# A vision block with a mixture of experts: shared network's first products from two fp32r parts, gates and state in place, three weights parted early

## What is computed

```python
h = attention(x)                        # 16 heads, softmax, output projection
h = concatenate([cls_tok, h])           # one class row in front of each sequence
h = h + state_space(layernorm(h))       # a linear recurrence over the rows, then C and D
u2 = layernorm(h)
shared = (silu(u2 @ Wg_s.T) * (u2 @ Wu_s.T)) @ Wd_s.T      # 256 -> 512 -> 256
p = sigmoid(u2 @ Wr.T + rb); two best of 8 experts
out = h + shared + sum(p_e * expert_e(u2))                 # experts of the same form as shared
```

## Time and profile before

| | |
|---|---|
| median of 3 runs | 1178.23 us (1177.75 to 1178.30) |
| the profiled execution | 1178.34 us, its span 1176.7 us |
| PE busy | 1131.6 us, 96% of the span |
| DVE busy | 908.8 us, 77% |
| ACT busy | 580.9 us, 49% |
| POOL busy | 400.1 us, 34% |
| mixing, from `make_y(1)` to `make_y(7)` | 543.49 to 761.68 us, six steps |

### The profile page before, as it was taken

The page is one execution under the profiler, slowest core; times in us unless marked ns, Lnnn a source line. Parts: engine busy times, 40 slices in busy tenths (PEclk is TensorE's granted clock), DMA queues, the critical chain, the costliest instruction groups (busy, mean ns, idle before and its releaser), DMA issues.

```text
span 1176.7 us, 21838 instructions
## 1 busy us (share of the span) xinstructions
PE 1131.6 (96%) x5894; PEld 685.5 (58%) x5895; DVE 908.8 (77%) x1557; ACT 580.9 (49%) x963; POOL 400.1 (34%) x516
## 2 busy tenths in 40 slices
PE   6998999999999999999999999987999999999996
PEld 3654333333333333466566766556888888888885
DVE  3788888888888888588877877777777777777775
ACT  3444777777777777632232221423444444444442
POOL 3011630101111010204345333464555555555553
PEclk9998999999999999999999999998999999999998
DMA  8886232323323232041244422411333333333332
GB/s 280 280 254 209 72 103 70 105 73 95 100 70 103 71 99 82 19 148 53 70 108 108 90 59 68 90 37 41 55 54 54 54 54 54 54 54 54 54 54 32
DMA packets 108690, 105.36 MB, mean 90 GB/s; under 512 B 42464, under 2 KB 97904, under 8 KB 108624
## 3 DMA queue, kind: packets, MB, share of 16 engines
q1 hardware_dynamic: 90528, 81.18, 24.2%
q0 software_dynamic: 18112, 23.57, 11.4%
HBM read 64.88 MB, written 39.68 MB: 89 GB/s over the span
## 4 chain that ended last, share of the span: by engine, by line
PE 79%; DVE 8%; issue 1%; ACT 1%; DMA 0%; POOL 0%; POOLq 0%; DVEq 0%
PE mix_pairs L73 17%; PE by_key L662 11%; PE pv L673 11%; PE by_query L653 9%; PE mix_made L1781 8%; PE mix_pairs L1251 5%; PE mix_pairs L1260 4%; PE mix_turn L1768 3%; PE mix_made L1236 2%; PE mix_made L1207 2%; PE mix_turn L1748 1%; PE mix_turn L1191 1%; PE by_query L694 1%; PE mix_made L1224 1%; DVE wu_rest L899 1%
## 5 line engine op out<-in xcount | busy, mean ns | idle before, releaser
L746 DVE TENSOR_REDUCE k_neg_max<-by_query 128x2 f32<-128x1024 f32 x240 | 282.9, 1220 | 54.7 <-PE by_query L653 54.0
L806 ACT ACTIVATE k_wu_e<-by_key 128x512 f32<-128x512 f32 x512 | 278.5, 601 | 84.0 <-PE by_key L662 80.5
L662 PE MATMUL by_key<-k_wg_e 99*128 99x512 bf16 x512 | 180.5, 386 | 3.1 <-DVE pv L782 3.0
L1724 POOL DMA_INDIRECT out_rows<-x_y,k_slot x72 | 113.9, 1582 | 157.7 <-PE mix_turn L1748 92.5
L653 PE MATMUL by_query<-k_wg_e 96*128 96x512 bf16 x480 | 145.0, 383 | 0.2
L1823 ACT ACTIVATE x_gate<-mix_pairs 128x512 f32<-128x512 f32 x72 | 43.0, 597 | 200.3 <-PE mix_pairs L73 200.3
L673 PE MATMUL pv<-k_wu_e,k_wd_e 128*17 128x512 f32 x1024 | 134.5, 598 | 0.3 <-ACT k_wu_e L806 0.3
L662 PEld LDWEIGHTS by_key<-k_wg_e 99*128 99x128 bf16 x512 | 42.4, 97 | 144.3 <-ACT k_wu_e L806 81.0
L73 PE MATMUL mix_pairs<-w_short,x_T 128*128 x288 | 121.8, 423 | 2.1 <-issue 2.1
L1781 PEld LDWEIGHTS mix_made<-x_wd,x_acts_T 128*128 128x128 f32 x864 | 111.2, 188 | 7.3 <-ACT x_acts_T L1845 0.9
L73 PE MATMUL mix_pairs<-w_short,x_rest 128*128 x288 | 114.8, 399 | 0.0
(11 more groups left out here) (234 smaller groups left out, 1851.9 us busy)
## 6 DMA issues: line engine op xcount, KB each, us to landing
k_wg_e<-kept_qk SPq DMA_DIRECT2D x384, 64.0 KB, 2.1
kept_qk<-k_qk_parts SPq DMA_DIRECT2D x32, 384.0 KB, 3.5
kept_v<-k_v_ones SPq DMA_DIRECT2D x8, 544.0 KB, 5.5
k_wd_e<-kept_v SPq DMA_DIRECT2D x32, 136.0 KB, 2.6
k_wu_e<-in_xT POOLq DMA_DIRECT2D x8, 512.0 KB, 6.2
kept_heads<-k_wd_e SPq DMA_DIRECT2D x8, 512.0 KB, 2.9
k_heads_in<-kept_heads SPq DMA_DIRECT2D x8, 512.0 KB
k_wg_e<-in_wg_e SPq DMA_DIRECT2D x8, 512.0 KB, 4.6
```

The source lines that it names most:

```text
L662: pe.matmul(by_key[:, key_bank(job), :], k_rows[0:SROWS, g, h, kt * P:(kt + 1) * P], q_rows[0:SROWS, g, h, :], start=True, stop=True).then ...
L746: dve.tensor_reduce(neg_max[:, g % 2, 2 * n:2 * n + 2], by_query[:, bank:bank + 2, :], AX.X, ALU.max, negate=True).then_inc(query_read, 1)
L806: act.activation(probs[:, key_tile(j) // 2 * G + j // 2 % G, j % 2, :], by_key[:, key_bank(job), :], ACT.Exp, scale=float(HD) ** -0.5).the ...
L1724: pool.indirect_dma_start(out=dram["out"], in_=y[:, r % 2, :], in_offset=None, compute_op=ALU.add, out_offset=bass.IndirectOffsetOnAxis(ap ...
```

## The change

- `shared_up` takes `u2` and the shared weights in two fp32r parts: 12 records per chunk in place of 8. It gets two waits (`w_s_cut`, `u2_cut`).
- ACT makes `u2_short` straight from PSUM (`copy_turned`), DVE makes `u2_rest` by `cut_second`, also from PSUM, and only then ACT makes the fp32 `u2_T`, which the router still needs; the logits wait for both, since they are written where the transposed u2 lay.
- Once, in step 0: ACT shortens the two shared weights (2 x [128, 2, 512]), DVE cuts them, behind `first_sum(1)` and ahead of `class_add`.
- `act_T` is gone: `shared_act` writes over `gate`, and silu now waits for `down_made` of the batch before. `state` is gone: the scans write over `back`, and `make_hidden` has its products in another order; their number is the same.
- `EARLY` is 3: pieces 0 to 2 in steps 1 to 3. In step 7 ACT shortens 3 to 10 and DVE cuts 3 and 4; in step 8 DVE cuts 5 to 15, eleven pieces; ACT shortens 11 between silu 1 and silu 2 and 12 to 15 behind silu 3.
- Some semaphores are joined (`choice_steps`, `dma_begun`); buffers lie elsewhere.

```diff
-EARLY = 4
+EARLY = 3
@@ stage_mix
-        act_T = sb("mix_act_T", [P, FC, S], FP32)
+        w_s_short = sb("w_s_short", [P, 2, DC, F], FP32)
+        w_s_rest, w_s = mem["w_s_rest"], (mem["wg_s"], mem["wu_s"])
@@ scalar
             def silu(j, m):
                 act.wait_ge(ev["gate_made"], FC * j + m + 1)
-                act.wait_ge(ev["act_done"], FC * j)
+                act.wait_ge(ev["down_made"], 2 * j)
...
                 if last:
                     act.wait_ge(mem["experts_in"], 16 * 3 * (E - 2))
+                    shorten_weights(act, mem, 3)
+                    act.wait_ge(ev["out_made"], 2 * B)
                     shorten_weights(act, mem, 4)
-                    act.wait_ge(ev["out_made"], 2 * B)
-                    shorten_weights(act, mem, 5)
+                if not this:
+                    act.wait_ge(ev["u2_stored"], 16 * B)
+                    shorten_weights(act, mem, 11)
...
-                    for n in (6, 7, 8):
+                    for n in (5, 6, 7):
...
-                    act.wait_ge(ev["state_done"], 2 * B)
-                    shorten_weights(act, mem, 9)
                     act.wait_ge(ev["y_made"], 2 * B)
-                    for n in (10, 11, 12):
+                    for n in (8, 9, 10):
...
                 if this:
+                    copy_turned(short(u2_short), b, "u2_turned", "shared_shortened")
+                    act.wait_ge(ev["u2_cut"], b + 1)
                     copy_turned(u2_T, b, "u2_turned", "u2T_copied")
...
                 if not this:
-                    act.wait_ge(ev["u2_stored"], 16 * B)
                     act.wait_ge(ev["logits_made"], B)
-                    for n in (13, 14, 15):
+                    for n in (12, 13, 14, 15):
...
+            for n in range(2):
+                act.activation(short(w_s_short[:, n, :, :]), w_s[n][:, :, :], ACT.Copy).then_inc(ev["shared_shortened"], 1)
             batches(act, step)
@@ tensor, shared_up
                 if m == 0:
                     pe.wait_ge(ev["acc_done"], 2 * j)
+                    pe.wait_ge(ev["w_s_cut"], 2)
+                    pe.wait_ge(ev["u2_cut"], j + 1)
...
-                        mm = pe.matmul(pairs[:, m % 2, n, :], w[:, c, m * P:(m + 1) * P], u2_T[:, c, :],
-                                       start=(c == 0), stop=(c == DC - 1))
+                        mm = split_products(pe, pairs[:, m % 2, n, :],
+                                            (w_s_short[:, n, c, m * P:(m + 1) * P], w_s_rest[:, n, c, m * P:(m + 1) * P]),
+                                            (u2_short[:, c, :], u2_rest[:, c, :]), start=(c == 0), stop=(c == DC - 1))
@@ tensor, step
                     pe.wait_ge(ev["u2T_copied"], b + 1)
+                    pe.wait_ge(ev["u2_cut"], b + 1)
@@ vector
-                dve.tensor_tensor(act_T[:, m, :], gate[:, m, :], pairs[:, m % 2, 1, :], ALU.mult).then_inc(ev["act_done"], 1)
+                dve.tensor_tensor(gate[:, m, :], gate[:, m, :], pairs[:, m % 2, 1, :], ALU.mult).then_inc(ev["act_done"], 1)
...
+            def cut_second(b):
+                dve.wait_ge(ev["shared_shortened"], 2 + b + 1)
+                dve.tensor_tensor(short(u2_rest[:, :, :]), turn[:, :, :], u2_short[:, :, :],
+                                  ALU.subtract).then_inc(ev["u2_cut"], 1)
...
-                scan(dve.tensor_tensor_scan(state[:, 0, :], back[0], back[1], mem["state0"][:, 0:1],
+                scan(dve.tensor_tensor_scan(back[0], back[0], back[1], mem["state0"][:, 0:1],
                                             ALU.add, ALU.add), wait=False)
...
-                dve.tensor_tensor(back[0], state[:, 0, :], cos, ALU.mult)
-                scan(dve.tensor_tensor(back[1], state[:, 1, :], sin, ALU.mult))
                 dve.wait_ge(ev["y_made"], 2 * b)
-                dve.tensor_tensor(hidden[:, 0, :], back[0], back[1], ALU.subtract).then_inc(ev["state_done"], 1)
...
+                dve.tensor_tensor(back[1], back[2], sin, ALU.mult)
+                scan(dve.tensor_tensor(hidden[:, 0, :], back[0], cos, ALU.mult))
+                dve.tensor_tensor(hidden[:, 0, :], hidden[:, 0, :], back[1], ALU.subtract).then_inc(ev["state_done"], 1)
...
                     if not this:
-                        for n in (6, 7, 8, 9):
+                        for n in (5, 6, 7, 8):
                             cut_weights(dve, mem, n)
...
                     shared_add(b - 1, 1 - par, 1)
                     if not this:
-                        for n in range(13, 2 * E):
+                        for n in range(12, 2 * E):
                             cut_weights(dve, mem, n)
+                if this:
+                    cut_second(b)
                 if nxt:
                     first_sum(b + 1)
                 if not prev:
+                    dve.wait_ge(ev["cls_up"], 1)
+                    for n in range(2):
+                        dve.wait_ge(ev["shared_shortened"], n + 1)
+                        dve.tensor_tensor(short(w_s_rest[:, n, :, :]), w_s[n][:, :, :], w_s_short[:, n, :, :],
+                                          ALU.subtract).then_inc(ev["w_s_cut"], 1)
+                if not prev:
                     class_add()
                 if this and not nxt:
-                    for n in (4, 5):
+                    for n in (3, 4):
                         cut_weights(dve, mem, n)
```

More of the change, by code:

```diff
@@ L928, in stage_mix @@
         by_feature = "p (c t) n -> p c (t n)"
-        heads_T, u_T, state, hidden, u2_T = (mem["mix_" + n][:, :, :].rearrange(by_feature, c=DC)
-                                             for n in ("heads_T", "u_T", "state", "hidden", "u2_T"))
+        heads_T, u_T, hidden, u2_T, u2_short, u2_rest = (
+            mem[n][:, :, :].rearrange(by_feature, c=DC)
+            for n in ("mix_heads_T", "mix_u_T", "mix_hidden", "mix_u2_T", "u2_short", "u2_rest"))
         h2 = sb("mix_h2", [P, 2, TT, D], FP32)
@@ L1467, in step @@
                     dve.wait_ge(ev["sigmoid"], b)
-                    top_two(dve, chain(dve, ev["top_steps"], TOP_STEPS * (b - 1)), mem, probs[:, :, :], TT)
+                    top_two(dve, chain(dve, ev["choice_steps"], (TOP_STEPS + SLOT_STEPS + 2) * (b - 1)), mem, probs[:, :, :], TT)
                     dve.tensor_tensor(chosen[:, 0:TT, :], mem["hot"][:, :, 0, :], mem["hot"][:, :, 1, :],
@@ L1506, in step @@
                     if not this:
-                        for n in (10, 11, 12):
+                        for n in (9, 10, 11):
                             cut_weights(dve, mem, n)
@@ L1709, in gather @@
                 pool.wait_ge(ev["x_turned"], R * i + r - X + 1)
[L1710 removed]
+            pool.sem_inc(mem["dma_begun"])
             gather_x(pool, mem, dram, r)
@@ L1983, in program @@
                "ev_cut": {n: sem("weights_" + n) for n in ("shortened", "rest_made")},
-               "tiles_listed": sem("tiles_listed"), "adds_listed": sem("adds_listed"), "slot_in": [sem(f"slot_in{r}") for r in range(RING)],
+               "tiles_listed": sem("tiles_listed"), "dma_begun": sem("dma_begun"), "adds_listed": sem("adds_listed"), "slot_in": [sem(f"slot_in{r}") for r in range(RING)],
                "x_gathered": [sem(f"x_gathered{r}") for r in range(FIRST_X)]}
```

44 lines of the change are left out of this document (22 added, 22 removed).

## The result

Changed kernel: 1179.9 us, the median of 20 runs (1178.43 to 1182.62). Kernel before, on the same chip: 1178.38 us, the median of 20 runs (1175.98 to 1179.83). The ratio is 1.0015, with a 95% interval of 1.0008 to 1.0022. So it is slower by 1.5 us, inside the 0.2% that was counted as no change. The profiled execution took 1180.8 us, 0.9 above the median; its span is 1179.1.

A forecast was written before the change was run, and what follows sets the result against it. Each mixing step's cycle was taken to run through both PE and DVE, with only chunk 1 on it. Sum: 1178.34 + 5.7 + 2.0 - 8.1 + 3.3 = 1181.2 us; forecast's own range 1179.0 to 1183.5, overall 1174.8 to 1186.0.

The forecast's parts named there:

- The cycle: Middle steps run through PE and DVE, only chunk 1 on the cycle: 35.01 us a step, -8.1 in all.
- PE is what counts: Rival, chance 0.13: DVE's chain has hidden slack, steps fall towards PE's own 33.35, 1171.2 us.
- The cover called thin: Middle steps: ACT's u2_T copy ends at 4.25, the projection on PE at 4.32, so logits not late by 0.07 us.
- A record of 0.233: Shared network's chunks: fp32r records 0.233 us apart, 12 take 2.80, 0.63 less per chunk.
- The cut of u2: DVE's cut of u2 from PSUM in each step: 1.22 us, bounds 1.1 and 1.4.
- The cut that is there first goes first: Steps 1 to 3: weight cut comes 0.55 ahead of POOL's second product, its wait vanishes; otherwise 2.1 more in steps 2, 3.
- The hold of POOL's power in step 0: DVE's cuts in a row hold POOL's power until 528.1, delaying normalise: +5.7 us, with no hold +4.9.
- The clock at `make_y(1)`: New PE wait ahead of make_y(1) lowers the clock, a slow make_y: +2.0 us (0 to 2.8).
- the clock holds: Rival, chance 0.24: new waits leave the clock full, so the 2.0 and 0.8 go: 1178.4 us.
- The clock in each step: Rival, chance 0.03: waits of 0.85 and 0.56 drop the clock every step, 1.8 each, +10.8 over six: 1192.0 us.
- The end: Step 7 to the experts: open u2 chain, slow logits, shorter chunks behind count, an eleventh cut: sum +3.3 us.
- The 2.3 of the chain on u2: Step 7, no projection covers the cut and second copy ahead of the logits: +2.3 us, all open.

The follow-up runs named there:

- experiment 1: Changed kernel with only chunk 0 of the shared network's first products back to 8 fp32 records: 1178.45 us, 1.0002 to the kernel before.
- experiment 2: Changed kernel with only chunk 1 of the shared network's first products back to fp32: 1188.38 us, 1.0078 to the kernel before.
- experiment 10: Changed kernel with weight cuts sooner in step 0, logits sooner in step 7, bias ahead of normalise, plus unread PE products at five places: 1173.13 us.
- experiment 12: Changed kernel, no order altered, with unread PE products at five places (6, 8, 3, 6 and 13): 1177.43 us, 0.9995 to the kernel before.
- experiment 6: Changed kernel; in step 7 ACT copies fp32 u2_T first, logits wait for that alone, fp32r parts are made afterwards, DVE cuts weights meanwhile: 1175.82 us.
- experiment 7: Changed kernel with the router's bias put ahead of normalise of the next batch: 1179.13 us, 1.0012 to the kernel before.
- experiment 4: Changed kernel without the product of the weights' rest, 8 fp32r records a chunk in place of 12: 1181.08 us, 1.0024 to the kernel before.
- 5: Changed kernel with step 0's two cuts of shared weights moved ahead of cut_second and first_sum(1): 1180.10 us, 1.0018 to the kernel before.
- 9: Changed kernel with weight cuts sooner in step 0, logits sooner in step 7 and the bias ahead of normalise: 1176.06 us, 0.9981 to the kernel before.
- experiment 11: Kernel before the change with unread PE products at five places (4, 2, 4, 4 and 12): 1174.74 us, ratio 0.9975.
- experiment 8: Changed kernel with unread PE products, six ahead of make_y(1) and eight behind step 7's turn of u2: 1177.25 us, 0.9996 to the kernel before.

## Why the prediction was right, point by point

The forecast was 2.9 us more; the medians say 1.5 us more, the traced execution 2.5 us. That is inside the forecast's own range (1179.0 to 1183.5), at its lower end, and among the three outcomes it is "same" (given 0.36), not the "slower" that was held likelier (0.48). The mechanism of the middle steps is right; three terms around them are off and partly cancel.

- **The cycle** was right in mechanism and size. Experiments 1 and 2 show it: chunk 0 is worth 0.00 a step, chunk 1 0.65. The rival "PE is what counts" (0.13) falls with experiment 1: DVE's chain has no slack, `turn_input` waits 0.55 for the bias. The predicted wait there was 0.85. Of the 0.30 between them 0.07 is that `turn_input` came sooner, and 0.13 that the logits began later: ACT's second copy ended at 704.25, so they began 4.46 behind the turn, and 4.33 behind it before (705.02 and 700.69). The cover called thin was too short, which costs nothing, since it only eats into a wait. The last 0.1 is not traced. DVE's recurrence took 7.04 as said, from 717.02 to 724.06, so the new order of its products and the writes in place cost nothing.
- **A record of 0.233** was right: 710.84 to 711.08 is 0.24, and a chunk takes 2.87 up to the next product.
- **The cut of u2** (1.22, bounds 1.1 and 1.4): 1.22 in each step. It reads PSUM, and the indirect DMAs of POOL beside it took 0.97, their usual time.
- **"The cut that is there first goes first"** was right. DVE's and POOL's timeline of step 3 in the changed kernel, against the earlier trace rows:

```profile
610.35 1.57 DVE L899 TENSOR_TENSOR wg_rest<-k_wg_e,w_short 128x1024 fp32r<-128x1024 f32 x1 [0.26 <-ACT w_short L891]
...
610.92 3.27 POOL L1078 TENSOR_TENSOR mix_h<-mix_h,k_mix_h 128x1024 f32<-128x1024 f32 x1
```

  The cut is 0.57 ahead (0.55 was worked out), 1.57 long where it was 3.35, and POOL's product is the one that stretches. The 0.35 over 1.22 fits POOL's first product, which still ran when the cut was issued (608.49 to 610.85). The Trainium skill says the same ("SBUF — State Buffer", "Who interferes with whom"): an operation of VectorE with two inputs in SBUF contends with one of GpSimd that reads SBUF, and the one issued first keeps the port. The order of the cuts matters more than the prediction said: before, the three steps with a cut lasted 36.88 to 36.90 and those without 35.56 to 36.08, so by an estimate some 3 of the 8.6 us that the middle gained are the cuts' (the order of two and the absence of the third), not the chunks'.
- **The hold of POOL's power in step 0** was the step that failed, by 0.8 of the 1.0 us that this stretch was over: "POOL was held until a gap". The row behind it, an indirect DMA of 3.28, did span several cuts, and in experiments 10 and 12 one spans four. The power was let in after one cut, in the same kernel. A price for one operation of an engine did not carry to another one.
- **The clock at `make_y(1)`**: 1.2 and not 2.0, within the bounds 0 to 2.8. This term is not one number: with the same instructions up to there, `make_y(1)` took 5.16 in the changed kernel and 3.93 in experiment 6, behind waits of 2.62 and 1.63. The waits differ because chunk 0 of step 0 did: in experiment 6 all of its 12 records ran at the low clock (527.20 to 532.48), in the changed kernel only the first seven and part of the next, so PE came to its wait 0.8 sooner. At this place the traces fall in two groups: 3.92 or 3.93 behind waits of 1.03 to 1.88 (experiments 1, 2, 6, 7 and the kernel before), 5.16 to 6.55 behind 2.39 to 4.96 (the changed kernel, 4, 5, 9). Elsewhere the length of the wait does not decide: `make_y(2)` was slow behind 1.95 in experiment 2 and at full clock behind 2.61 in experiment 4. The rival "the clock holds" is thus true, at this place, of some executions and not of others.
- **The clock in each step** (0.03): no. Waits of 0.55 at two places cost nothing, in 34.93 us after 34.93. In experiment 4, with 1.47 at `turn_input` and 0.38 to 4.96 at `make_y`, two of six steps lose 1.5 to 2.1, those behind 4.96 and 1.80. The Trainium skill's "HAM oscillation" ("TensorE: Matmul & The Clock Gate") was weighed as a rival; the changed kernel's steps don't bear it out, and experiment 4 bears it out in two of six and not in each.
- **The end** was undersized: +5.6 for +3.3. The 2.3 of the chain on u2 was exact (2.31). The slow logits cost 1.64 (0.8 taken, 1.7 the upper bound). The chunks gave back 0.5 in place of 0.95, since eleven of the eighteen records behind `count` ran at the low clock. The eleventh cut was 1.1 as said. What the sum did not have is the last `shared_down`: its wait grew from 1.67 to 3.14, it ran slow, and DVE waited 0.77 for it, ahead of the cuts that set the experts' start. The working had named the wait's growth nowhere: it let PE finish its chunks sooner and did not ask who would use the time.
- The misses are -1.0, -0.8, -0.5, +2.3 and -0.55 and come to -0.55, so the sum is closer (1181.2 to 1180.8) than its terms, and closer to this execution than to the median (1179.9). That it landed is partly luck.
- **Against the expectations of the experiments**: the clock was expected to explain the difference of the two kernels ("the change looks better by 2 us"). That was not measured: with the unread products the changed kernel stands at 0.9995 and the one before at 0.9975, 0.0020 apart, and they were 0.0015 apart without. But the pair does not settle what the clock is worth either. The experts' first product comes at 808.96 in experiment 12 and at 808.83 in experiment 11: up to there the two kernels are equal. The 2.7 us between them lie in the experts' stage, which experiment 12 begins at the low clock, behind a wait that the unread products themselves brought about. What is shown is this: with the clock held in mixing, step 0 (+4.9) and the end (+3.9) still take back what the middle gains (-8.7). At the end it is the open chain of step 7, as experiment 6 shows, and in experiment 12 also the late gather. The best order with unread products (experiment 10, 0.9950 to 0.9977) and the kernel before with them (0.9964 to 0.9985) are not told apart.
- **What no run tried**: `EARLY` went from 4 to 3, and this moved a cut from step 4 to the end, where it costs 1.1. The steps with a cut are now as long as those without, so the traces suggest that a fourth early cut would be free. That is an estimate, and whether the memory allows it is not shown.

## What to carry to other kernels

Ask of each saved cycle which wait ends last beside it: here chunk 1 paid in full (0.65 a step) and chunk 0 not at all, and the 20 us that left PE in 32 chunks shortened the middle by less than nine. Look again, in a loop's first and last round, at every order that its middle hides: the open chain of step 7 cost 3.5 us, more than two middle steps saved. Where PE waits at a place at which its next work is on the path, a sooner input or a few unread products can be worth more than less work (experiments 6 and 8 gained more than experiment 4), but then look at what the earlier finish collides with.

## What the hardware did that was not expected

- Less work on PE did not make it faster. Experiment 4 has 8 records of 0.233 in place of 12 and is at 1.0024 (1.0013 to 1.0035), where the changed kernel is at 1.0015; the mean granted clock fell from 0.983 to 0.973. Adding 14 unread products, some 6 us (experiment 8), made the changed kernel faster by 2 to 3 us, and 26 of them made the kernel before faster by 3.2.
- The same code met another clock in another execution. `make_y(1)` took 5.16 in the changed kernel and 3.93 in experiment 6, with the same instructions ahead of it.
- An indirect DMA on POOL took 4.79 us beside a run of four cuts on DVE (0.96 in the changed kernel), while POOL's power was let in behind the first of two. The Trainium skill ("SBUF — State Buffer", "Who interferes with whom") infers that the generation of descriptors does not wait for such a two-input operation; the rows at 802.02 and the earlier trace rows speak against it, and the measurement decides. Whether it is the reading of the slots that is held, or the writing of descriptors, no run tells.
- DVE's bias, when it was put ahead of `normalise`, never started before POOL's power was about to end, and in six steps of 18 waited up to 1.6 us longer, for a release that the trace only calls remote. No run settled what it is.
